# Narrow attentions of a vision tower: a GpSimd multiply, a new order on ScalarE and VectorE, more products of constants

## What is computed

```python
q, k, v = split(x @ qkv_w.T + qkv_b)            # 12 heads of 16
q, k = rms_norm(q, q_norm_w), rms_norm(k, k_norm_w)   # block 0 only
w = softmax(einsum('bhnd,bhmd->bhnm', q, k) / sqrt(16))
out = einsum('bhnm,bhmd->bhnd', w, v) @ proj_w.T + proj_b
# block 3 besides: "quantum" weights over whole tokens, mixed in by a gate
sp = x @ sp_w.T + sp_b; re, im = halves of sp / norm
fid = ov_re**2 + ov_im**2;  quantum_out = softmax(fid) @ x
return sigmoid(qw) * quantum_out + (1 - sigmoid(qw)) * out
```

## Time and profile before

| | us |
|---|---|
| median of 3 runs | 916.25 |
| lowest and highest | 909.3, 916.74 |
| the profiled execution | 915.89 |
| its span, first to last instruction | 914.1 |

### The profile page before, as it was taken

The page is one execution under the profiler, slowest core; times in us unless marked ns, Lnnn a source line. Parts: engine busy times, 40 slices in busy tenths (PEclk is TensorE's granted clock), DMA queues, the critical chain, the costliest instruction groups (busy, mean ns, idle before and its releaser), DMA issues. The chain is left out here.

```text
span 914.1 us, 16334 instructions
## 1 busy us (share of the span) xinstructions
PE 836.3 (91%) x5892; PEld 602.5 (66%) x5893; DVE 431.5 (47%) x894; ACT 353.3 (39%) x785; POOL 183.5 (20%) x206
## 2 busy tenths in 40 slices
PE   6888979999999899999989879998999799989997
PEld 5565656677776457777758556765687467765786
DVE  5567376777852612222249576771104464742111
ACT  2355443444533022232325565444151433432342
POOL 0550002445600024444310002000000200001232
PEclk9989699999987799999999899999999877997999
DMA  8021100000002967212133001673000143503111
GB/s 300 5 35 20 20 2 1 1 2 2 1 1 59 260 188 214 73 43 52 35 90 97 1 1 29 132 175 82 1 1 1 20 101 70 115 1 108 36 52 36
DMA packets 80141, 56.21 MB, mean 62 GB/s; under 512 B 53254, under 2 KB 73256, under 8 KB 80076
## 3 DMA queue, kind: packets, MB, share of 16 engines
q1 hardware_dynamic: 71644, 41.26, 18.5%
q0 software_dynamic: 4416, 9.84, 3.9%
q10 hardware_dynamic: 4016, 4.23, 1.4%
HBM read 45.96 MB, written 9.35 MB: 61 GB/s over the span
## 5 line engine op out<-in xcount | busy, mean ns | idle before, releaser
L79 PE MATMUL banks<-con 128*128 128x512 f32 (+1 forms) x192 | 93.1, 597 | 3.0 <-DVEq L2254 1.4
L1964 PE MATMUL banks<-moe_wu,moe_xf 96*128 x256 | 90.9, 499 | 1.7 <-ACT moe_xf L2072 0.9
L1964 PEld LDWEIGHTS banks<-moe_wu,moe_xf 96*128 96x128 f32 x256 | 46.8, 192 | 31.2 <-issue 4.2
L154 ACT ACTIVATE ln_sq<-x 96x544 f32<-96x544 f32 x32 | 21.0, 656 | 104.6 <-DVE x L146 104.5
L687 PE MATMUL banks<-x,a_wqkv 96*96 96x272 f32 x192 | 55.2, 438 | 0.0
L79 PEld LDWEIGHTS banks<-con 128*128 128x128 f32 x192 | 38.1, 215 | 25.4 <-issue 22.1
L2269 DVE TENSOR_TENSOR moe_hid<-banks,moe_gs 128x384 f32<-128x384 f32 x32 | 17.8, 558 | 75.8 <-PE banks L1964 75.8
L1201 DVE TENSOR_TENSOR a_kx<-a_k,con 96x1632 f32<-96x1632 f32 x24 | 46.2, 1930 | 9.5 <-ACT a_k L991 9.0
L2126 POOL DMA_INDIRECT moe_xs<-moe_x_rows,moe_taken x32 | 31.3, 979 | 75.9 <-PE banks L1948 52.6
L164 PE MATMUL banks<-ln_sq,con 96*96 96x272 f32 x128 | 39.6, 436 | 5.3 <-ACT ln_sq L154 5.2
L687 PEld LDWEIGHTS banks<-x,a_wqkv 96*96 96x96 f32 x192 | 34.4, 184 | 14.9 <-issue 5.4
(11 more groups left out here) (412 smaller groups left out, 1760.4 us busy)
## 6 DMA issues: line engine op xcount, KB each, us to landing
moe_wu<-in_moe_up SPq DMA_DIRECT2D x16, 576.0 KB, 4.7
f_w<-in_f_e SPq DMA_DIRECT2D x10, 576.0 KB, 8.3
moe_wd<-in_moe_down SPq DMA_DIRECT2D x16, 288.0 KB, 5.6
patch_px<-in_patches SPq DMA_DIRECT2D x4, 768.0 KB, 9.5
a_vt<-a_v_rows SPq DMA_DIRECT2D x72, 36.0 KB
a_v_rows<-a_vtok SPq DMA_DIRECT2D x24, 96.0 KB, 1.8
f_wu<-in_f_up SPq DMA_DIRECT2D x4, 576.0 KB
f_wd<-in_f_down SPq DMA_DIRECT2D x4, 576.0 KB
```

Of the source, the lines that this page charges most:

```text
L79: self.nc.tensor.matmul(self.ps[bank][:, 0:width], self.ident, self.con[:, 0:width], start=True, stop=True)
L154: nc.scalar.activation(env.sq[:, c % 2], chunk(self.x, c), ACT.Square).then_inc(self.squared, 1)
L1964: last = nc.tensor.matmul(ps[2 + 2 * p + u][:, 0:BW], xf[0:KU[a], p, a], wu[0:KU[a], bass.ds(e, 1), a, u * BW:(u + 1) * BW].rearrange("p e ...
```

## The change

- Tokens stage: one product of constants more before the last `ln.var`.
- Narrow attentions, TensorE: the product of constants after the second `turn_weights` of chunk 0 has 512 and not 256 columns in a3; one of 256 columns is new between the last two `turn_weights`.
- ScalarE: in a0 `take_weights(2c+1)` goes before the fourth `take`; `ln.square(c-1)` and `first_rms.square` go from before the third `head_rms`, `take_inputs` and `take_context(2c)` to behind the fourth `head_rms`; at the end `exponent(2L+1)` goes behind `take_weights(2L)`.
- VectorE: `scale_context(2c)` goes before `total(2c+1)`, `ln.centre(c-1)` before the second `spread_keys`; in a0 the first `head_scale` goes before `scale_context(2c)` and `spread_keys(c+1, 0)` is gone; at the end `ln.centre` goes before the last `total`.
- GpSimd: in a0 the first half of the keys of chunks 1 to 3 is spread there; the response's part 1 waits for chunk 0's second spread; in a3 the `vt` buffers are cleared only after the fifth gate step.
- Routed experts: 5 and 2 products for 3 and 1 (moe and f3) before the ranks, 7 for 6 in moe before the lists, 7 and 6 for 3 and 3 before the first rows, 8 for 6 at moe's end. Convolution: 2 new products before the seventh `turn_weights`.

```diff
@@ stage_tokens, TensorE
+            env.idle_products(1, 4)
             ln.var(pe, NC - 2)
@@ stage_narrow_attention, TensorE
-                    env.idle_products(1, 0, 256)
+                    env.idle_products(1, 0, 512 if quantum else 256)
...
             turn_weights(2 * L)
+            env.idle_products(1, spare, 256)
             turn_weights(2 * L + 1)
@@ ScalarE
-                take(c + 1, 3)
-                take_weights(2 * c + 1)
-                if not rms and not quantum and c + 2 < NC:
-                    take_values(c + 2)
-                if first_rms is not None and c == NC - 2:
-                    first_rms.square(act, 0)
-                if c >= 1:
-                    ln.square(act, c - 1)
-                if rms:
+                    take_weights(2 * c + 1)
+                    take(c + 1, 3)
                     head_rms(NT * (c + 1) + 2)
+                else:
+                    take(c + 1, 3)
+                    take_weights(2 * c + 1)
                 if quantum:
                     take_inputs(2 * c + 1)
+                elif not rms and c + 2 < NC:
+                    take_values(c + 2)
                 take_context(2 * c)
                 if rms:
                     head_rms(NT * (c + 1) + 3)
+                if c >= 1:
+                    ln.square(act, c - 1)
+                if first_rms is not None and c == NC - 2:
+                    first_rms.square(act, 0)
...
-            exponent(2 * L + 1)
             if quantum:
                 take_inputs(2 * L)
             take_weights(2 * L)
+            exponent(2 * L + 1)
             take_weights(2 * L + 1)
@@ GpSimd
+            if quantum:
+                pool.wait_ge(gate_step, 5)
             for c in range(2):
                 pool.memset(vt_rows[:, c], 0.0).then_inc(vt_zero, 1)
-                if c == 0 and response is not None:
-                    response.on_pool(pool, 1)
+            if response is not None:
+                pool.wait_ge(k_spread[1], 1)
+                response.on_pool(pool, 1)
+            for c in range(1, NC if rms else 0):
+                pool.wait_ge(qk_ready, NT * c + 1)
+                if c >= 2:
+                    pool.wait_ge(scored, GPC * (c - 1))
+                nc.gpsimd.tensor_tensor(kx[:, c % 2, 0]..., k[:, c % 2, 0]..., env.head_mask..., ALU.mult).then_inc(k_spread[0], 1)
@@ VectorE
                 total(2 * c)
-                if not rms:
-                    spread_keys(c + 1, 0)
-                total(2 * c + 1)
                 if rms:
                     head_scale(c + 1, 0)
+                else:
+                    spread_keys(c + 1, 0)
                 scale_context(2 * c)
+                total(2 * c + 1)
...
                 if rms:
-                    spread_keys(c + 1, 0)
                     head_scale(c + 1, 1)
-                spread_keys(c + 1, 1)
                 if c >= 1:
                     ln.centre(dve, c - 1)
+                spread_keys(c + 1, 1)
...
             total(2 * L)
+            ln.centre(dve, L - 1)
             total(2 * L + 1)
-            ln.centre(dve, L - 1)
@@ stage_routed_ffn, TensorE
-            env.idle_products(3 if top2 else 1, 0)
+            env.idle_products(5 if top2 else 2, 0)
...
-            env.idle_products(6 if top2 else 2, 0)
+            env.idle_products(7 if top2 else 2, 0)
...
-            env.idle_products(3, 3)
+            env.idle_products(7 if top2 else 6, 3)
...
-                env.idle_products(6, 3)
+                env.idle_products(8, 3)
@@ stage_convolution, TensorE
             for n in range(4, len(turns)):
+                if n == 6:
+                    env.idle_products(2, 7)
                 turn_weights(n)
```

More of the change, by code:

```diff
@@ L1181, in _ @@
                 pool.memset(tiny[:, 1:2], 1e-8).then_inc(pad_zero, 1)
+            if quantum:
+                pool.wait_ge(gate_step, 5)
             for c in range(2):
                 pool.memset(vt_rows[:, c], 0.0).then_inc(vt_zero, 1)
-                if c == 0 and response is not None:
-                    response.on_pool(pool, 1)
+            if response is not None:
[5 more added lines that the diff above has]
+                    pool.wait_ge(scored, GPC * (c - 1))
+                nc.gpsimd.tensor_tensor(kx[:, c % 2, 0].rearrange("p i (k h) -> p i k h", h=HH),
+                                        k[:, c % 2, 0].rearrange("p (i k) -> p i k", k=N)[:, :, :, None].broadcast_to([HD, IC, N, HH]),
+                                        env.head_mask[:, None, None, :].broadcast_to([HD, IC, N, HH]), ALU.mult).then_inc(k_spread[0], 1)
         @block.vector
```

## The result

| | before | after |
|---|---|---|
| median of the paired runs | 912.77 us (4 runs) | 873.21 us (4 runs) |
| lowest and highest | 901.76, 916.74 | 871.51, 874.96 |
| profiled execution, its span | 915.89, 914.1 | 874.83, 873.0 |

The change is faster: the ratio is 0.9627, with a 95% interval of 0.9581 to 0.9672 (it leaves out the slowest executions of the kernel before, so it lies above the ratio of the two medians). The direction was forecast, the size was not: 888.5 us with a range from 879 to 903, and 873 came. Over the runs of the experiments the kernel before has a median of 908.4 us (59 executions, 898.8 to 917.9); the changed one, with the four of the table, has 874.1 (14, 870.9 to 878.2). So 34.3 us were gained where 27.3 were forecast, and the sum had been laid against an execution 7.5 us above the median: 7.0 and 7.5 make up the miss of 14.4, but for rounding.

The account below looks back on a forecast made before the run. TensorE, busy nine tenths or more, was taken to set the pace, losing time to short waits and the low clock behind them. Terms 16.8 + 17.8 - 1.7 - 2.1 - 3.5 = 27.3 off 915.9 gave 888.5 us, range 879 to 903.

Parts of the forecast that it names:

- The base: Starting time of the sum: profiled execution of 915.89 us, 0.4 below the median, so both usable alike.
- a0, chunk 1: TensorE's wait at 92.5 us in a0: 2.2 and 0.6 of waiting plus 7.4 of clock, 10.2 us gained.
- Start of a0 and chunk 0: Response behind the first two spreads in a0: 2.0 us of idle and 1.3 of clock, 3.3 gained (0 to 5).
- Chunk 2: In a0, TensorE's wait mostly stays, now for first_rms.square; 1.4 us gained with the clock (0 to 3).
- the end of a0: Later exponent(7), earlier ln.centre and some clock at a0's end: 0.5 us gained (-1.5 to 2).
- a3's start: GpSimd's memsets behind gate_step in a3: 3.6 us of TensorE's idle and 2.3 of clock, 5.9 gained.
- Context scaling: In a3, scale_context(0) before total(1) lets TensorE turn the contexts earlier: 1.6 us gained.
- The clock of 743 to 763: Low clock stretch of 20.5 us in a3, worth 9.8 us, of which 9.2 was taken as gained.
- the clock falls all the same: Rival: both long stretches of a0 and a3 stay low, 7.4 and 9.2 us not gained, 905 us; chance 0.14.
- a2: Attention stage without such a wait can only lose: late scores, late ln.var and the end cost 1.7 us (0 to 3).
- Products: Added products of constants: moe loses 2.1 us, f3 3.5, convolution and moe's end 0; the tokens stage gains 1.4.
- the products cost little: Rival: expert products cost little or give clock back, moe 0 and f3 -1, 882 us; chance 0.14.

## Why the prediction was wrong in size

By its own steps, in its order:

1. *The base.* "0.4 below the median, so the two can be used alike": this step failed, and it is the largest part of the miss. Three runs within 0.8% looked like a narrow kernel; 59 executions spread over 2.1%, and the median of the three lay 7.8 us above theirs. 7.5 us of the miss.
2. *a0, chunk 1*, 10.2: the traces show 10.5, with `values` waiting 0.67 where I said 0.7. Right, and the run with the old orders shows its cause.
3. *Start of a0 and chunk 0*, 3.3: between the traces 5.8, of which undoing the response's move takes back 4.9 (5.6 in the medians). Failed, because I let the late multiply and the response take back most of the clock, and because the 0.8 that the new order takes off the wait for the turned weights was in chunk 1's sum and not in chunk 0's. The multiply was scaled from a row of 512 elements (4.0 us) and took 3.04.
4. *Chunk 2*, 1.4: 1.9, and *the end of a0*, 0.5: 1.4, both inside their bounds. The sum for a0 between the traces is 19.6 where its terms say 15.4, and alone a0's part brought 20.3.
5. *a3's start*, 5.9: 6.4 in the trace. *Context scaling*, 1.6: 1.8. *take_inputs*, 1.1: 1.2, both right by mechanism. *The clock of 743 to 763*, 9.2: 9.1 between the two traces, but only two of the four traces with that wait had it to give. a3's part is 14.3 and not 17.8. I had the rival "the clock falls all the same" for the kernel after; what I didn't ask is whether it always falls in the kernel before.
6. *a2*, -1.7: -1.8 in the traces, so right in size; but the chunks' order, to which I gave 1.4 of it, gave back only 0.2 when undone.
7. *Products*, -5.6, with 1.4 for tokens: -0.6 together with a2, so 1 us or so gained without it where the terms say 4.2 lost. This step failed. The tokens stage did give 1.6 between the two traces (a0's first matmul at 39.16 for 40.75), but in the four other traces without the new product there it stands at 39.4 to 39.7: that fall, too, was one execution's, and the product is worth nothing that these traces show. f3's 3.5 stood (2.4 by the traces). moe's 2.1 was too dear, since the clock that the products hold up shortens what follows (-0.8 in most traces); what the convolution's and moe's last products give no run shows apart. The nearest of my rivals is "the products cost little", to which I gave 0.14; it had f3 at -1, which f3 was not.

Laid against the median of 908.4 the same sum gives 881, 7 above what came. With a0's part as measured (4.9 more), a3's (3.5 less) and the rest (5.3 more) it gives 874.4. That a3's surplus and part of the others' shortfall cancel is luck.

## What to carry to other kernels

Where the clock falls behind a wait, take a second trace of the kernel before, or the spread of many times, before booking the fall in full: a wait is there in each execution, the fall behind it may not be. The long stretches at the low clock are worth more than the waits that they stand behind, and an order of small operations on the helper engines (the one that TensorE waits for goes ahead of the one that itself waits) removes such a wait. It is not free everywhere: a2, which had no such wait, lost 1.8 us. A multiply moved to GpSimd pays if it meets few two-input operations of VectorE, and the order on VectorE must be made for it.

## What the hardware showed that I had not expected

- The same wait of 2.12 or 2.13 us in a3 was followed by 21 us at the low clock in two traces and by none in two. In a0 waits of 2.3 and 2.9 us were followed by a fall in each of four, and the wait of 2.13 at chunk 2 by one of some 4 us in ten traces of eleven.
- GpSimd's multiply of 1632 elements against a broadcast mask took 3.04 us, 1.9 ns for an element, where the earlier trace rows has 2.5 ns for an element of one of 512.
- A VectorE operation with two inputs waits for the whole of a multiply on GpSimd: 3.27 us in place of 0.49 when that took 3.40, with both ends 0.30 apart. The Trainium skill ("SBUF — State Buffer", Who interferes with whom) calls it a lock for a whole instruction, and the trace agrees.
- A clear on GpSimd holds VectorE's `tensor_scalar` of four elements for 4.04 us, up to the end of the second clear, lets one of a single element pass in 0.15, and leaves a `tensor_tensor` of 1632 elements alone (1.81).
